# A fused two-layer graph network: the next graph's key products and normed tiles move from the third head pair into the first two, in two PSUM banks that hold sums

## The reference

```python
h = maximum(layernorm(x), 0)
q, k, v = heads(h @ Wq + bq), heads(h @ Wk + bk), heads(h @ Wv + bv)   # 6 heads of 64
x = x + merge(softmax(q k^T / 8 + mask) v) @ Wf + bf
h = maximum(layernorm(x), 0)
hh = h @ W                                                            # 12 heads of 32
a = leaky(tanh(hh) w_src + (tanh(hh) w_dst)^T, 0.2), masked, softmax
f = elu(a hh + b)
g = sigmoid(h @ H_w^T + H_b)
x = x + g * f + (1 - g) * h
```

## Time and profile before

| | |
|---|---|
| median of 3 runs | 1792.91 us (1792.54 to 1793.63) |
| the profiled execution, its own time | 1793.03 us |
| its span, first to last instruction | 1791.2 us |
| mean granted TensorE clock | 0.991 of full |
| busy: PE, DVE, ACT, POOL | 1667.4, 1315.1, 1102.8, 1033.5 us |
| one graph, between equal places of two graphs | about 108.3 us |

### The profile page before, as it was taken

How to read it: one execution, slowest core, us unless ns; L and a number is a source line. 1 busy time by engine, 2 the same in 40 slices (tenths; PEclk the granted TensorE clock), 3 DMA queues, 4 the chain that set the end, 5 groups by cost and what they waited for, 6 DMA issues and landing times.

```text
span 1791.2 us, 34573 instructions
## 1 busy us (share of the span) xinstructions
PE 1667.4 (93%) x12528; PEld 1016.4 (57%) x12528; DVE 1315.1 (73%) x3130; ACT 1102.8 (62%) x2231; POOL 1033.5 (58%) x1287
## 2 busy tenths in 40 slices
PE   6899999999999999999999999999998999999885
PEld 4474655647465574655647456474655746556452
DVE  4678687786877768687786877768777786876756
ACT  3666565665666656566665666656566665656653
POOL 3456565664656656565565656656575565655645
PEclk9899999999999999999999999999999999999997
DMA  4000101001010010101001010010100101000000
GB/s 156 19 19 11 50 7 37 22 8 50 7 54 7 15 40 8 54 7 36 18 12 50 7 37 25 6 49 7 54 7 19 36 12 50 7 19 19 6 14 18
DMA packets 38248, 48.24 MB, mean 27 GB/s; under 512 B 2624, under 2 KB 38080, under 8 KB 38080
## 3 DMA queue, kind: packets, MB, share of 16 engines
q1 hardware_dynamic: 38080, 46.03, 8.0%
HBM read 33.44 MB, written 12.58 MB: 26 GB/s over the span
## 4 chain that ended last, share of the span: by engine, by line
PE 74%; DVE 12%; ACT 6%; issue 6%; POOL 1%; DMA 0%; DVEq 0%; SPq 0%; POOLq 0%
PE work L1106 19%; PE score L1106 16%; PE acc L1264 7%; PE acc L1196 6%; PE acc L1258 5%; PE score L1163 4%; PE work L1179 4%; ACT arena L575 4%; DVE sm L821 3%; PE work L1258 3%; PE score L1239 2%; DVE arena L866 2%; DVE arena L831 2%; PE acc L1217 2%; PE score L1121 2%
## 5 line engine op out<-in xcount | busy, mean ns | idle before, releaser
L866 DVE SCALAR_TENSOR_TENSOR arena<-score,uqT,adjT 128x512 f32<-128x512 f32 x576 | 389.2, 744 | 42.2 <-PE score L1239 31.7
L418 POOL TENSOR_SCALAR arena<-arena,rinv 128x512 f32<-128x512 f32 x384 | 282.2, 749 | 226.6 <-DVE rinv L827 226.6
L575 ACT ACTIVATE arena<-sm,nmax 128x512 f32<-128x512 f32 x384 | 273.5, 714 | 140.5 <-DVE nmax L821 138.7
L452 POOL TENSOR_TENSOR arena<-arena,adjT 128x512 f32<-128x512 f32 x192 | 223.9, 1166 | 130.8 <-ACT arena L616 121.8
L821 DVE CUSTOM_DVE_ANT_0 sm<-score,mask 128x512 f32<-128x512 f32 x384 | 247.6, 685 | 62.0 <-issue 30.2
L1196 PE MATMUL acc<-arena,v_tok 128*64 128x512 f32 x768 | 200.7, 614 | 11.2 <-DVE arena L831 9.6
L1179 PEld LDWEIGHTS work<-ident_f,arena 64*128 64x128 f32 x3072 | 113.8, 139 | 168.0 <-DVE arena L831 89.3
L425 POOL TENSOR_TENSOR rstd<-var,mhalf 128x1 f32<-128x1 f32 x128 | 68.7, 549 | 242.8 <-DVE var L785 242.8
L1264 PE MATMUL acc<-arena,u_den 128*3 128x512 f32 x1536 | 200.4, 592 | 0.0
L831 DVE COPY arena<-work 128x512 f32<-128x512 f32 x192 | 131.4, 684 | 82.2 <-PE work L1179 81.1
L613 ACT ACTIVATE arena<-score,nqT 128x512 f32<-128x512 f32 x192 | 130.2, 678 | 86.6 <-PE score L1239 59.0
(11 more groups left out here) (168 smaller groups left out, 3935.9 us busy)
## 6 DMA issues: line engine op xcount, KB each, us to landing
x_in<-in_x SPq DMA_DIRECT2D x16, 768.0 KB, 4.6
xb<-in_x SPq DMA_DIRECT2D x16, 768.0 KB, 4.7
out_x<-xres SPq DMA_DIRECT2D x64, 192.0 KB, 1.9
adj_u<-in_adj SPq DMA_DIRECT2D x16, 256.0 KB, 2.8
arena<-in_wk SPq DMA_DIRECT2D x1, 576.0 KB, 6.8
arena<-in_wq SPq DMA_DIRECT2D x1, 576.0 KB, 7.9
arena<-in_wv SPq DMA_DIRECT2D x1, 576.0 KB, 9.3
arena<-in_wf SPq DMA_DIRECT2D x1, 576.0 KB, 10.2
```

Of the source, the lines that this page charges most:

```text
L418: nc.gpsimd.tensor_scalar(pr, pr, rinv[:, p, t, i:i + 1], 1.0, ALU.mult, ALU.mult).then_inc(probs_ready, 1)
L452: nc.gpsimd.tensor_tensor(edge_at(n, HG - 1), t_ring[:, n % 2], adjT[:, n % TT], ALU.mult).then_inc(last_edge_ready, 1)
L575: nc.scalar.activation(probs[p % 2 * 2 + i][:, t], sm[:, n % NSM], ACT.Exp, scale=-1.0, bias=nmax[:, p, t, i:i + 1], accum_out=rsum[:, p, ...
L866: nc.vector.scalar_tensor_tensor(out=edge_at(n, j), in0=score[j][:], scalar=uqT[:, c, q:q + 1], in1=adjT[:, c], op0=ALU.max, op1=ALU.mult) ...
```

## The change

Four things change, and with them the queues of ACT, DVE and POOL that must follow.

1. `shared` grows to eight banks: 6 is `acc[1]` and 7 is `acc[0]`. Normed tiles 0 and 3 go to bank 6, tiles 1 and 2 to banks 2 and 3. Key product 0 goes to bank 7.
2. Normed tiles 0 and 1 now come after turn (0, 1) and context (0, 0), tile 2 after context (0, 1), tile 3 after context (0, 3). Key product 0 comes after context (1, 0), key product 1 after context (1, 3), so ahead of turn (2, 0); key product 2 stays. Context (1, 0) waits until normed tile 3 is drained, context (2, 0) until key product 0 is, and key product 0 until the sums of pair 1 are taken out.
3. In the tail `values(3)` moves ahead of sums 1. Sums 0 to 3 now use banks 0, 1, 4 and 5.
4. ACT makes `exps(1, 0)` after `pT_copy(0, 0)` instead of before it. Graph 0 has places of its own (`HOME_0`): normed tiles 0 and 1 both in bank 2.

```diff
-    ("k", 0): 2, ("k", 1): 3, ("k", 2): 5, ("q", 0): 1, ("q", 1): 4, ("q", 2): 1,
+    ("k", 0): 7, ("k", 1): 3, ("k", 2): 5, ("q", 0): 1, ("q", 1): 4, ("q", 2): 1,
...
-    ("num", 1): 0, ("fin", 0): 0, ("fin", 1): 0, ("fin", 2): 1, ("fin", 3): 1,
-    ("norm1", 0): 2, ("norm1", 1): 3, ("norm1", 2): 4, ("norm1", 3): 5,
+    ("num", 1): 0, ("fin", 0): 0, ("fin", 1): 1, ("fin", 2): 4, ("fin", 3): 5,
+    ("norm1", 0): 6, ("norm1", 1): 2, ("norm1", 2): 3, ("norm1", 3): 6,
+HOME_0 = {("norm1", 0): 2, ("norm1", 3): 5, ("k", 0): 4}
-NORM_AFTER = {(0, 2): (0, 1), (1, 2): (2, 3)}
-KEY_AFTER = {(2, 0): 1}
-KEY_BEHIND = {1: 0, 2: 2}
+NORM_BEHIND = {(0, 1): (0, 1), (0, 2): (2,), (0, 3): (3,)}
+KEY_BEHIND = {(1, 1): 0, (1, 3): 1, (2, 3): 2}
-        shared = work + score
+        shared = work + score + [acc[1], acc[0]]
 # PE, attention
                         for tile in S_AFTER.get((p, c), ()):
                             scores(g, *tile)
+                        if c > 0:
+                            context(g, p, c - 1, more)
+                        if c == TT - 1:
+                            context(g, p, c, more)
                         if more:
-                            for t in NORM_AFTER.get((p, c), ()):
+                            for t in NORM_BEHIND.get((p, c), ()):
                                 turn_norm(g + 1, 0, t)
...
 # PE, tail of layer2
                     scores(b + 1, 0, 3)
+                    values(b + 1, 3)
                 turn_sums(b, 1)
                 turn_sums(b, 2)
-                if more:
-                    values(b + 1, 3)
                 turn_sums(b, 3)
 # DVE, pair 3
-                pT_copy(g, 2, 0)
+                ctx_low(g, 1)
                 if fin:
                     difference(g - 1, 2)
                     positive(g - 1, 3)
-                if more:
-                    qk_low(g + 1, 0, "k")
+                pT_copy(g, 2, 0)
+                if more:
+                    qk_low(g + 1, 1, "k")
                 pT_copy(g, 2, 1)
-                ctx_low(g, 1)
 # POOL: add_out(g - 1, 0) moves from before normalise(g, 2, 0) to before normalise(g, 2, 3)
```

More of the change, by code:

```diff
@@ L81, in attention_order @@
                 order += both("s", *tile)
[L82 to L86, removed]
+            order += [("norm1", t) for t in NORM_BEHIND.get((p, c), ())]
+            if (p, c) in KEY_BEHIND:
+                order += [("k", KEY_BEHIND[p, c])]
     return order
@@ L107, with home @@
 FIRST = [(0, x) for x in START_UP] + [(ahead(x) - 1, x) for x in attention_order()]
+def home(g, *name):
+    return HOME_0.get(name, HOME[name]) if isinstance(g, int) and g == 0 else HOME[name]
 def place(g, *name):
-    bank = HOME[name]
-    first = [x for x in FIRST if HOME[x[1]] == bank]
+    bank = home(g, *name)
+    first = [x for x in FIRST if home(x[0], *x[1]) == bank]
     turn = [x for x in TURN if HOME[x] == bank]
@@ L466, in attention @@
                     normalise(g, 1, t)
+                for t in range(TT - 1):
+                    normalise(g, 2, t)
                 if fin:
                     add_out(g - 1, 0)
-                for t in range(TT):
-                    normalise(g, 2, t)
+                normalise(g, 2, TT - 1)
                 if fin:
@@ L627, in attention @@
                 pT_copy(g, 0, 0)
+                exps(g, 1, 0)
+                pT_copy(g, 0, 1)
                 exps(g, 1, 1)
-                pT_copy(g, 0, 1)
                 exps(g, 1, 2)
                 pT_copy(g, 0, 2)
[L632 to L635, removed]
                 if more:
@@ L638, in attention @@
                     turned_high(g + 1, 0, 1)
[L639 to L646, removed]
+                exps(g, 1, 3)
+                pT_copy(g, 0, 3)
                 if more:
                     turned_high(g + 1, 0, 2)
+                ctx_high(g, 0)
+                if more:
                     turned_high(g + 1, 0, 3)
+                pT_copy(g, 1, 0)
+                exps(g, 2, 0)
+                pT_copy(g, 1, 1)
+                exps(g, 2, 1)
+                exps(g, 2, 2)
+                if fin:
+                    elu(g - 1, 0)
+                if more:
+                    qk_hi_copy(g + 1, 0, "k")
+                pT_copy(g, 1, 2)
+                pT_copy(g, 1, 3)
                 exps(g, 2, 3)
-                pT_copy(g, 1, 3)
                 if fin:
@@ L908, in attention @@
                 inverse(g, 1, 2)
+                if more:
+                    turned_low(g + 1, 0, 0)
+                    turned_low(g + 1, 0, 1)
+                pT_copy(g, 0, 3)
+                inverse(g, 1, 3)
+                if more:
+                    turned_low(g + 1, 0, 2)
+                maxima(g, 2, 0)
+                pT_copy(g, 1, 0)
+                ctx_low(g, 0)
+                if more:
+                    turned_low(g + 1, 0, 3)
+                inverse(g, 2, 0)
+                maxima(g, 2, 1)
+                pT_copy(g, 1, 1)
+                maxima(g, 2, 2)
+                inverse(g, 2, 1)
                 if fin:
@@ L912, in attention @@
                     positive(g - 1, 0)
-                pT_copy(g, 0, 3)
-                inverse(g, 1, 3)
+                inverse(g, 2, 2)
+                pT_copy(g, 1, 2)
                 if fin:
@@ L917, in attention @@
                 if more:
[L918 to L929, removed]
+                    qk_low(g + 1, 0, "k")
+                maxima(g, 2, 3)
+                pT_copy(g, 1, 3)
                 if fin:
                     positive(g - 1, 1)
-                maxima(g, 2, 3)
-                inverse(g, 2, 2)
-                if more:
-                    turned_low(g + 1, 0, 2)
-                    turned_low(g + 1, 0, 3)
-                pT_copy(g, 1, 3)
                 inverse(g, 2, 3)
@@ L1041, in layer2 @@
                 divide(b, 1)
+                if more:
+                    inverse(b + 1, 0, 3)
                 inverse_den(b, 2)
                 divide(b, 2)
-                if more:
-                    inverse(b + 1, 0, 3)
                 inverse_den(b, 3)
@@ L1183, in turn_probs, with context @@
                                 mark_full(ins, b, "turn", p, c, half)
-            def context(b, p, c):
+            def context(b, p, c, more):
                 if p == 0 and c == 0:
@@ L1191, in context @@
                     pe.wait_ge(ctx_ready, b * NPAIR + 1)
+                if more and p > 0 and c == 0:
+                    drained(pe, b + 1, *(("norm1", 3), ("k", 0))[p - 1])
                 for i in range(2):
```

39 lines of the change are left out of this document (15 added, 24 removed).

## The result

The changed kernel takes 1807.1 us against 1793.1, each the median of four runs. One of its four runs took 3233 us; it is left out of the ratio, which is 1.0077 with a 95% interval of 1.0057 to 1.0097, and the other three lie between 1806.4 and 1807.7. The forecast was 1765, with a range of 1754 to 1780. The profiled execution has a span of 1804.7 us, 13.5 more than before, and a mean granted clock of 0.977 where it was 0.991.

What follows compares the result with a forecast made beforehand. The kernel was taken as a PE queue with gaps. 14 graphs at 1.7 us = 23.8, last attention 1.5, start and graph 0 together 0, end 2.4: 27.7 off 1793.0 gives 1765 us, range 1754 to 1780.

Steps and rivals of the forecast that it cites:

- The tail: End of layer 2: values 3 no longer waits 1.47 us; of the 1.5 us, 1.4 arrive at turn (0, 0).
- the first copies: Start of attention: maxima (1, 0) 1.2 us earlier, turn (0, 1) at 596.85 instead of 598.75, PE 1.9 us ahead.
- the normed tiles: Two tiles moved into pair 1, costing some 0.8 us there: turn (1, 0) starts at 606.2 instead of 606.86.
- the walk: DVE's and ACT's queues followed item by item at measured durations: 2.8 us of waits against 4.96, about 2.2 gained per graph.
- I take 0.5 per graph: Loss where POOL's add_out meets DVE's positive and difference, bounds 0 and 1.7 us in pair 3; leaves 1.7 gained per graph.
- rival B: Middle graphs: the walk holds as it stands, 14 x 2.2 + 3.9 = 35 us gained, 1758 us; chance 0.2.
- The clock (D): Pair 3 at half speed in its 6.5 us, up to 4 us lost per graph, 1825 us; chance 0.02.
- the collisions (A): POOL and DVE collide in full: pair 3 loses 1.2 us instead of 0.5, copy (1, 3) 0.2 more; 1778 us; chance 0.18.
- Wrong: Signs against: idle at context (1, 0), turns waiting for POOL, idle over 2.5 at turn (2, 1), clock under 1.00 in pair 3.
- The ends: Outside the middle graphs: start and graph 0 together 0, last attention 1.5 us gained, last sums 2.4 gained.
- C: Turn (2, 1): its DVE copy waits for a chain of handovers; late by 3 us it gives 1800 us; chance 0.04.
- E: Pairs 2 and 3: waits for the same DVE work grow by what the tail gave, 1791 us; chance 0.04.

Runs made afterwards that it cites:

- The tail alone: Kernel before with only values 3 ahead of sums 1, sums in banks 0, 1, 4, 5, and DVE's inverse (0, 3) one place earlier: 1773.9 us, ratio 0.9896.
- the kernel without POOL's part: Changed kernel with POOL's add_out cut to 8 of 384 columns in all attentions: 1763.6 us, ratio 0.9836.
- the filled wait: Changed kernel with nine useless 128x512 products between turn (2, 0) and turn (2, 1): 1787.2 us, ratio 0.997.
- the kernel with the old tail: Changed kernel with values 3 again behind sums 2 and the sums in banks 0 and 1: 1826.4 us, ratio 1.019.
- that kernel: Changed kernel with key product 1 again behind turn (2, 0) instead of ahead of it: 1798.6 us, ratio 1.0035.

## Why the prediction was wrong

*The tail, the first copies, the normed tiles, key product 0, context (1, 3):* right. The starts of PE in the walk are met to 0.3 us down to turn (2, 0), the thin slack at context (1, 0) held, and context (1, 3) is 0.53 us late (0.7). The tail alone gave 1773.9 where the same walk gave 1773. The walk as a whole is confirmed by the kernel without POOL's part: its graph takes 106.2 us, 2.1 less than before, where the walk had 2.2.

*The step that failed* is "I take 0.5 per graph, since only the rest of a POOL operation is waited for". The collisions cost 1.7 us per graph: the copy of turn (2, 0) starts 1.72 us late. The reason given was true, but the rest was two thirds of the operation and more: `difference(2)` and `positive(3)` begin 0.34 and 0.26 us behind the start of a POOL operation, so neither missed, and they lost 1.26 us. `positive(1)` had met `add_out(0)` in the same way, and that came down the chain to `ctx_low(1)` as another 0.44. That the sum is the 1.7 which stood as the upper bound is luck, since that bound was for two instructions alone. Nor was there a middle between hit and miss to be taken: the order repeats, and the collisions are the same in all 14 middle graphs. Taking POOL's part out gives 1763.6 us, and putting the copy ahead of the two instructions 1767.1. The first belongs beside rival B's 1758, a walk without collisions, and the second has another order of DVE's queue: that both lie near the forecast says nothing for it. The Trainium skill (page "SBUF — State Buffer", section "SBUF: two separate sides") has the engine that comes second blocked for the other's whole instruction. The trace agrees: 1.07 and 1.35 us against 0.55 and 0.56 with `add_out` cut, each ending 0.42 us behind the POOL operation that it met.

*The second error is in the rivals.* The clock (D) had a chance of 0.02 as an event of its own, and the collisions (A) 0.18. But A makes the long wait, and the long wait halves the clock. The case in which both hold had no time worked out, and it was the one that came; both of its signs stood under "Wrong". I had set pair 2's 1.9 us of gaps at 1.00 against D; its longest single wait was 0.96 us, and it said nothing of one of 2.5. The row of graph 0 with 0.89 was the one to look at. The kernel before, graph 0, a wait from the timeline of PE and then the stretch around it:

```profile
53.62 0.37 PE L1179 MATMUL work<-ident_f,arena 64*128 64x64 f32 x2 [2.26 <-POOL arena L418]
```

```profile
53.00:58.00 5.00, 4.38 (x34) 3.61 (x36) 4.41 (x13) 3.68 (x10) 0.56 (x1) 0.50 0.01 2
```

This is the second of two waits over 2 us there, and PE is at 1.2 GHz for the whole of the stretch. D's price of 4 us was too high: 1.4 to 1.5 per graph by the filled wait and by the two stretches.

The sum in its true sizes: the walk's 2.2 us, less 1.7 for the copies, less 1.5 for the clock, is 1.0 lost per graph. Twelve of the 14 middle graphs lose 0.5 to 1.1, most of them 0.9; 0.15 us of wait at turn (2, 2), which the kernel without POOL's part has, is gone in them. One graph kept its clock and gained 0.6, and one lost 2.7 us to the clock in place of 1.5 and is 1.9 longer than before. Together that is the 11.7.

*The ends* were sized wrong too, by 5.7 us: a gain of 3.9 was forecast, and 1.8 was lost. The first product came 0.8 us later and not 1.5, but graph 0 gave back only 0.1 of it. The last sums gained 2.7 (2.4). The last attention was to gain 1.5; it lost some 4, with a wait of 2.97 us at turn (2, 1) and half clock behind it.

*Rivals:* C named the right place, turn (2, 1). Its chain through `ctx_high(1)` was late, but by 0.44 us of the 2.4 that it needed, and because of a collision. (By its own sum it needed more: with the 3.9 us of the ends, slower would have shown only from 2.7.) E is refuted by the tail alone.

*What stays open:* why one graph of 14, and 7 of 14 in the kernel with the old tail, keep their clock over the same wait. Where the half clock begins differs as well: in the graph of 627.43 turn (2, 1) itself is slow (1.08 us), in the one of 1609.90 it is not (0.71), and the next turn is (1.12).

## What to carry to other kernels

Work that is only there to be done, like `positive` and `difference` here, belongs behind the copy that the matrix engine waits for, above all where GpSimd runs beside it. Don't price a collision by half: where the order repeats, the collision may come in every round, as here in all 14 graphs, so lay the two queues side by side and price it in full where they meet. When cover is taken from a place, ask how long the single wait there can get, and price that wait together with the half clock behind it, as one case. Where a wait can't be avoided, any matmuls in it may pay.

## What the runs showed of the hardware that was not expected

- The same 2.5 us wait of PE was followed by half clock in 13 graphs of 14 and by full clock in one, with the same work around it: 10.53 and 9.05 us. With the old tail it was 7 and 7.
- A VectorE instruction of 0.55 us with two SBUF inputs that began while a GpSimd `tensor_tensor` ran ended 0.40 to 0.43 us behind it, whatever was left of that one: 0.87 to 1.35 us in all (rows of the changed kernel).
- Nine useless products of 128x512 in the wait made the kernel 20 us faster (1807.1 to 1787.2).
- Two waits of 0.89 and 0.50 us close together were followed by half clock too, in 10 of 14 graphs, and the runs of that kernel spread over 10.8 us, those of the kernel before over 3.
